# Two rounds of graph message passing on one core: node stages in blocks of 128 nodes instead of 125

## The chip, the cores and the metric

The kernel runs on one core of a Trainium2 chip. The metric is the device time of one execution in microseconds (us), median of the runs shown. The core has five engines that run side by side and wait for each other through semaphores: TensorE (PE in the profile, PEld is its weight load), VectorE (DVE), ScalarE (ACT), GpSimd (POOL) and SyncE (SP, which here only issues transfers). Transfers between the chip's main memory and the on-chip memory of 128 partitions are carried out by the core's 16 DMA engines.

## The reference

`N` = 6250 nodes with 128 features, `E` = 200000 edges sorted by destination.

```
def L0(x):                                   # attention, 4 heads of 32 channels
    xh    = x @ W
    alpha = leaky_relu(xi . a_i + xj . a_j)  # per edge and head, xi = xh[dst], xj = xh[src]
    alpha = softmax of alpha over the edges of one dst
    return segment_sum(xh[src] * alpha, dst)

def L1(x):                                   # three layers, l = 0..2
    h = emb, from layer 1 on normalised over the nodes (gamma, beta)
    w = sigmoid(relu([h[dst], h[src]] @ linA_w.T + linA_b) @ linB_w.T + linB_b)
    prop = segment_sum(w * h[src], dst)
    emb = relu([h, prop] @ lin_w.T + lin_b)
    return emb @ final_w.T + final_b         # after the three layers

x = layernorm(x + L0(x));  return layernorm(x + L1(x))
```

## The kernel before

Two kinds of stages alternate. **Edge stages** walk over 392 groups of 512 edges (`NG` groups, `U` = 8 buffers). For each group POOL issues four indirect gathers of 128 rows of 1 KB each (function `gather`, line 594) from a table in main memory: `T0` (`gat_rows`) in the attention round, `T1` (`mp_rows`) in each of the three layers. SP fetches a window of per-destination data for the group (lines 491 and 548). PE, DVE and ACT work on the group behind them. POOL may be 8 groups ahead: gather `k` waits until group `k - 8` has been used and until ACT has copied its indices (line 669).

**Node stages** walk over the nodes in `N / NB` = 50 blocks of `NB` = 125 nodes, in turns of `BU` = 5 or `BL` = 10 blocks. `node_steps` staggers the sub-steps of a stage over successive blocks, and buffers rotate over 5 slots. A block has its nodes either in the partitions (tiles `[0:NB, ...]`) or in the columns (`[:, ... NB]`). In order of time:

- **Load.** ACT's queue loads `x` into `xall` in five transfers (line 646). SP loads the two edge lists, as 97 partitions of 2048 edges (line 424) and one short row (line 425), and then 23 weight transfers (lines 432 to 449), the last of them parts of `params`. DVE waits for both edge lists (line 892), and computes what the groups need up to line 932; PE waits for all weights before it transposes anything (line 1494), the transposed edge lists go back through DVE (lines 911). Then POOL clears `acc` and `mh` (lines 584, 585), and DVE starts the table stage (line 939).
- **Table of the attention round.** Per block: copy (DVE, line 939), transpose and matmul (PE, 1521 and 1526), copies (ACT 659, 663), results into slot `u` of `tbl` (DVE, 947 to 951), one store of the block's rows to `T0` (SP, line 468), and per turn one store of small rows to `SI` (line 470). The first gather waits for all 50 stores.
- **Normalisation after the attention round.** Here SP loads `x` again by block (`load_x`, line 513) into 5 slots.
- **Per layer, table `T1`.** DVE normalises a block (1299), PE multiplies and transposes it (1637, 1638), ACT and DVE write its rows into `acc` (775, 1306); SP stores five blocks at a time to `T1` (line 527). The first gather of the layer, and ACT in the next stage, wait for all ten stores, since the next stage writes over `acc`.
- **Per layer, table `A3`.** DVE 1316, PE 1648, ACT 789, DVE 1324, ACT 793, DVE 1329; SP stores five blocks at a time to `A3` (`mp_dst_rows`, line 534). When all ten stores have landed, DVE clears `acc` (line 1340) and starts the edge stage. POOL's first 8 groups of gathers run beside this stage.
- **End.** After the third layer 50 blocks are finished, and SP stores each (line 570).

The stores and loads of the node stages have the block's nodes as their first dimension, for example:

```
sp.dma_start(T1[bass.ds(it * (NB * BL) + half * NB * BU, NB * BU), :].rearrange("(b n) c -> n b c", n=NB),
             rows_all[0:NB, row(it, half * BU, TW, 0, BU * TW)].rearrange("n (b c) -> n b c", c=TW))
```

Of the kernel before, what the change touches and what calls it, by code (L numbers as in the profile page):

```python
# [20 lines left out]
P = 128  # L21
T = 4
GE = P * T
W = 32
S = 3
H = 4
U = 8
NB = 125
BU = 5
# [13 lines left out]
PREP_IDENT = 10  # L43
PREP_CONST = PREP_IDENT + 13
PREP_REL = PREP_CONST + 5
# [8 lines left out]
def reached(k0, off, n, done=None):  # L54

    if done is not None and not done["ahead"]:
        return False  # L60
    return not isinstance(k0, int) or k0 + off >= n
# [30 lines left out]
def gnn_kernel(nc, x, src, dst, W0, att, linA_w, linA_b, linB_w, linB_b, lin_w, lin_b, gamma, beta, final_w, final_b,  # L92
# [3 lines left out]
    L = linA_w.shape[0]  # L96
    assert D == P and N % (NB * BU) == 0 and N % (CH * BU) == 0
    CQ = 4
    QP = -(-E // (GE * CQ))
    NG = QP * CQ  # L100
    assert NG % U == 0 and QP <= P and L * 4 * D + D <= U * T * 2 * D - N // NB * D
    QW = GE * CQ
    QF = E // QW
    NT = N // (NB * BU)
    CT = N // (CH * BU)
    NA = N + W
    TW = 2 * D
    AC = max(NA, N // NB * TW // 2)
    C = D // H
# [6 lines left out]

    T0 = nc.dram_tensor("gat_rows", (N, TW), F32, kind="Internal").ap()
    SI = nc.dram_tensor("gat_si", (NA * H, 1), F32, kind="Internal").ap()
    T1 = nc.dram_tensor("mp_rows", (N, TW), F32, kind="Internal").ap()
    A3 = nc.dram_tensor("mp_dst_rows", (NA, S * D), BF16, kind="Internal").ap()  # L120
# [5 lines left out]
    with ExitStack() as ctx:  # L126
        def sb(name, shape, dt=F32):
            return ctx.enter_context(nc.sbuf_tensor(name, shape, dt))

        def sem(name):  # L130
            return ctx.enter_context(nc.semaphore(name))
# [3 lines left out]

        xT = sb("xT", [P, N])
        mh = sb("mh", [P, NA])
        acc = sb("acc", [P, 2, AC])
        hT = mh[:, 0:N]

# [117 lines left out]
        bn = sb("bn", [P, 2])  # L258
        zeros = sb("zeros", [W, H])
        zeros16 = sb("zeros16", [W, S * D], BF16)  # L260

# [16 lines left out]
        more_copied = sem("more_copied")  # L278
        pads_stored = sem("pads_stored")
        acc_cleared = sem("acc_cleared")  # L280
# [91 lines left out]
        def nodes(turn, off, per=BU):  # L372

            return bass.ds(turn * (per * NB) + off * NB, NB)
# [46 lines left out]
        def _(sp):  # L421
            sp.wait_ge(pads_filled, 2)
            for tile, lst in ((dstI, dst), (srcI, src)):
                sp.dma_start(tile[0:QF, :], lst[0:QF * QW].rearrange("(q e) -> q e", e=QW)).then_inc(edges_loaded, 16)
                sp.dma_start(tile[QF:QF + 1, 0:E - QF * QW],  # L425
                             lst[QF * QW:E].rearrange("(q e) -> q e", q=1)).then_inc(edges_loaded, 16)
# [4 lines left out]
            with nc.allow_non_contiguous_dma(reason="columns of small weights"):  # L431
# [13 lines left out]
                for l in range(L):  # L445
                    sp.dma_start(params[:, l, C_LB:C_LB + 1], col(lin_b[l, :])).then_inc(weights_loaded, 16)
                    if l < L - 1:
# [11 lines left out]

            sp.dma_start(A3[N:NA, :], zeros16[:, :]).then_inc(pads_stored, 16)  # L460
            sp.dma_start(SI[N * H:NA * H, :].rearrange("(n h) o -> n (h o)", h=H),
                         zeros[:, :]).then_inc(pads_stored, 16)

            with sp.Fori(0, NT) as it:
# [17 lines left out]
            sp.wait_ge(rel16_stored, 16)  # L483
            sp.wait_ge(pads_stored, 32)
            sp.wait_ge(si_out, 16 * NT)
# [23 lines left out]
            def load_x(turn, off):  # L509
                n, u = turn * BL, off % BU  # L510
                if reached(n, off, BU):
                    sp.wait_ge(ln_y, n + (off - BU + 1))
                sp.dma_start(xrows[0:NB, u, :],
                             x[nodes(turn, off, BL), :]).then_inc(x_in[u], 16)

            sp.wait_ge(gat["acc"], NG)
            node_steps(sp, NT // 2, ((0, load_x),), BL)

# [47 lines left out]

            with sp.Fori(0, NT) as it:
                for u in range(BU):
                    sp.wait_ge(f_out, it * BU + (u + 1))
                    sp.dma_start(out[bass.ds(it * (NB * BU) + u * NB, NB), :],  # L570
                                 xblk[0:NB, u, :]).then_inc(out_done[u], 16)
            for u in range(BU):
                sp.wait_ge(out_done[u], 16 * NT)

        @block.gpsimd
        def _(pool):
            pool.iota(iotaI, pattern=[[1, IW]], base=0, channel_multiplier=0).then_inc(iotas_made, 1)
            pool.iota(pI[:, 0:1], pattern=[[1, 1]], base=0, channel_multiplier=1).then_inc(iotas_made, 1)

            pool.wait_ge(prep, PREP_MORE)
# [61 lines left out]
        def _(act):  # L643

            for n in range(BU):
                act.dma_start(xall[0:NB, n * NT:(n + 1) * NT, :], x[n * NT * NB:(n + 1) * NT * NB, :]
                              .rearrange("(b p) c -> p b c", p=NB)).then_inc(x_in[n], 16)

            for l in range(L):
# [204 lines left out]
        def _(dve):  # L854
# [30 lines left out]
            then(v.memset(negbig[:, :], -BIG))  # L885
            then(v.memset(zeros[:, :], 0.0))
            then(v.memset(zeros16[:, :], 0.0))
            then(v.memset(bn[:, 0:1], 1.0))
# [3 lines left out]

            dve.wait_ge(edges_loaded, 64)
            then(v.tensor_copy(dstF, dstI))
# [60 lines left out]
            for u in range(BU):  # L955
                dve.wait_ge(x_in[u], 16)
            node_steps(dve, NT, ((0, table_x), (3, table_rows)))

# [789 lines left out]
```

## Time and profile before

| what | value |
|---|---|
| median of 3 runs | 8660.34 us (8657.73 to 8661.98) |
| the profiled execution: its own time, its span | 8661.07 us, 8659.3 us |
| busy: PE, DVE, ACT, POOL | 57%, 58%, 16%, 70% of the span |
| mean granted TensorE clock | 0.515 of full speed |
| chain that ended last, by engine | POOL 46%, issue 23%, DMA 11%, DVE 7%, PE 7% |
| moved by DMA | 1075.13 MB, mean 124 GB/s |

Busy shares are averages over stages of different kinds. In the edge stages POOL issues one gather after the other; in the node stages it issues none. The DMA share of a stretch is the mean busy share of the 16 DMA engines, so one engine busy all the time shows as 0.06, and five as 0.31.

### The profile page before, as it was taken

The page shows a single profiled execution, that of the slowest core. Times are in us where ns is not written, and L with a number is a line of the kernel's source. Part 1 is how long each engine was busy: PE and PEld are TensorE (multiplying, and loading weights), DVE is VectorE, ACT ScalarE, POOL GpSimd, SP SyncE. Part 2 cuts the span into 40 slices and gives each one's busy share as a digit, 9 for nine tenths or more (in the row PEclk, how much of TensorE's full clock was granted, in tenths as well). Part 3 has the DMA queues.
Part 4 walks back from the last instruction along what each step waited for, and adds up shares of the span by engine and source line. Part 5 has one row for each costly group of instructions (what it writes and reads, how often), then busy time and mean ns, then how long its engine had stood idle before and what let it go on. Part 6 is the DMA issues. An engine that isn't in the chain of part 4 may idle for free.

```text
span 8659.3 us, 148704 instructions
## 1 busy us (share of the span) xinstructions
PE 4952.0 (57%) x27078; PEld 4216.4 (49%) x27079; DVE 5035.3 (58%) x26803; ACT 1412.8 (16%) x5406; POOL 6049.8 (70%) x6331
## 2 busy tenths in 40 slices
PE   2778788787654455445455554454455545544556
PEld 1667666676644444444444444444444444444445
DVE  4777777777655555555545555555555555555555
ACT  1333333333410000000030000000003000000002
POOL 1777777777367777777737777777773777777774
PEclk7555555555555555555565555555556555555555
DMA  2444444444244444444434444444443444444443
GB/s 77 126 127 128 127 128 127 127 128 127 84 131 130 129 129 130 129 129 130 130 102 127 129 130 130 129 129 130 129 119 110 130 130 129 130 129 129 129 130 93
DMA packets 752117, 1075.13 MB, mean 124 GB/s; under 512 B 323329, under 2 KB 550727, under 8 KB 751531
## 3 DMA queue, kind: packets, MB, share of 16 engines
q0 software_dynamic: 301056, 822.48, 33.0%
q1 hardware_dynamic: 444492, 246.95, 11.3%
q10 hardware_dynamic: 6275, 3.20, 0.1%
q14 instruction: 283, 2.32, 0.1%
q8 instruction: 11, 0.18, 0.0%
HBM read 1027.49 MB, written 44.53 MB: 124 GB/s over the span
## 4 chain that ended last, share of the span: by engine, by line
POOL 46%; issue 23%; DMA 11%; DVE 7%; PE 7%; SPq 2%; DVEq 1%; POOLq 1%; ACT 1%; ACTq 0%
POOL G L594 46%; DMA G<-mp_rows,idx 7%; DMA G<-gat_rows,idx 2%; DVE junk L1376 2%; PE ps L1577 2%; PE ps L1672 1%; PE ps L1537 1%; SPq L534 1%; SPq L527 1%; DMA gat_rows<-ring 1%; DMA mp_rows<-acc 1%; PE ps L1574 0%; SPq L425 0%; PE ps L1564 0%; PE ps L1648 0%
## 5 line engine op out<-in xcount | busy, mean ns | idle before, releaser
L594 POOL DMA_INDIRECT G<-mp_rows,idx x4704 | 4448.6, 946 | 1807.6 <-issue 1323.1
L1672 PE MATMUL ps<-selw,G 128*128 128x32 f32 x9408 | 2222.3, 400 | 596.4 <-DVE selw L1385 595.6
L1672 PEld LDWEIGHTS ps<-selw,G 128*128 128x128 f32 x9408 | 2093.9, 328 | 878.5 <-issue 760.7
L1365 DVE TENSOR_TENSOR pen<-ps,G 128x512 f32<-128x512 f32 x1176 | 812.7, 691 | 2728.2 <-DMA G<-mp_rows,idx 2724.5
L1662 PE MATMUL ps<-awin,ring 96*128 96x128 bf16 x4704 | 715.1, 307 | 2387.0 <-DVE ring L1350 2387.0
L594 POOL DMA_INDIRECT G<-gat_rows,idx x1568 | 1561.7, 996 | 552.6 <-issue 530.7
L1662 PEld LDWEIGHTS ps<-awin,ring 96*128 96x128 bf16 x4704 | 410.1, 132 | 2540.6 <-DVE ring L1350 2540.6
L802 ACT ACTIVATE gate<-logit,cur 128x4 f32<-128x4 f32 x1176 | 349.6, 297 | 5395.0 <-DVE junk L1376 5363.0
L1376 DVE SCALAR_TENSOR_TENSOR junk<-pen,ps 128x128 f32<-128x128 f32 x4704 | 1060.3, 278 | 0.1
L1350 DVE TENSOR_TENSOR ring<-ring,ps 96x512 bf16<-96x512 bf16 x1176 | 795.6, 677 | 0.4
L1577 PE MATMUL ps<-sel,weighted 128*128 128x32 f32 x3136 | 750.8, 404 | 0.0
L1577 PEld LDWEIGHTS ps<-sel,weighted 128*128 128x128 f32 x3136 | 698.0, 327 | 25.3
L1537 PE MATMUL ps<-ident,G 128*128 128x128 f32 x1568 | 428.4, 429 | 333.8 <-DMA G<-gat_rows,idx 332.1
L681 ACT ACTIVATE pen<-ring,negbig 128x512 f32<-128x512 bf16 x392 | 282.8, 721 | 1210.2 <-DVE ring L987 1210.2
L1537 PEld LDWEIGHTS ps<-ident,G 128*128 128x128 f32 x1568 | 280.6, 217 | 355.4 <-issue 207.1
L1013 DVE CUSTOM_DVE_ANT_0 junk<-ps,pen 128x512 f32<-128x512 f32 x392 | 268.1, 684 | 285.1 <-PE ps L1537 144.6
L1376 DVE DVE_READ_ACCUMULATOR junk<-pen,ps 128x1 f32 x4704 | 370.2, 79 | 0.0
L1355 DVE TENSOR_TENSOR ps<-ps,rel_all 128x128 f32<-128x128 f32 x1176 | 335.2, 285 | 0.0
L1385 DVE TENSOR_TENSOR selw<-ps,gate 128x128 f32<-128x128 f32 x1176 | 331.8, 282 | 0.2
L669 ACT COPY idx<-idx_all 128x4 int32 (+1 forms) x1572 | 284.5, 182 | 42.7 <-issue 42.2
L1122 DVE TENSOR_TENSOR weighted<-G,weighted 128x512 f32<-128x512 f32 x392 | 270.6, 690 | 0.0
L697 ACT ACTIVATE weighted<-al 128x512 f32<-128x512 f32 x392 | 246.5, 629 | 104.7 <-DVE al L1093 101.1
(182 smaller groups left out, 5074.3 us busy)
## 6 DMA issues: line engine op xcount, KB each, us to landing
ring<-rel_dst SPq DMA_DIRECT2D x1176, 96.0 KB
G<-mp_rows,idx POOLq DMA_INDIRECT x4704
ring<-rel_dst SPq DMA_DIRECT2D x392, 128.0 KB
awin<-mp_dst_rows SPq DMA_DIRECT2D x1176, 24.0 KB
G<-gat_rows,idx POOLq DMA_INDIRECT x1568
mp_rows<-acc SPq DMA_DIRECT2D x30, 625.0 KB
mp_dst_rows<-acc SPq DMA_DIRECT2D x30, 468.8 KB
sm<-gat_si SPq DMA_DIRECT2D x392, 0.5 KB
```

Of the source, the lines that this page charges most:

```text
L594: pool.indirect_dma_start(out=G[:, u, width * t:width * (t + 1)], out_offset=None, in_=table, in_offset=bass.IndirectOffsetOnAxis(ap=idx[: ...
L669: nc.scalar.copy(idx[:, T * (off % U):T * (off % U) + T], idx_all[:, bass.ds(k0 * T + off * T, T)]).then_inc(idx_ready, 1)
L802: nc.scalar.activation(gate[:, off % 4, :], logit[:, off % 4, :], ACT.Sigmoid, bias=cur[:, C_BB:C_BB + 1]).then_inc(done["gate"], 1)
L1350: v.tensor_tensor(selT16[0:S * W, off % 4, :], relbc16[0:S * W, off % 4, :], nodeP[0:S * W, :].to_broadcast([S * W, GE]), ALU.is_equal).th ...
L1355: v.tensor_tensor(selP[:, off % 4, :].rearrange("p (t n) -> p t n", t=T), iotaP.unsqueeze(1).to_broadcast([P, T, W]), rel4, ALU.is_equal). ...
L1365: v.tensor_tensor(pen[:, off % 2, :].rearrange("p (t c) -> p t c", t=T), PS[off % 2][:, :].rearrange("p (t c) -> p t c", t=T), Grows[:, of ...
L1376: v.scalar_tensor_tensor(junk[:, P * t:P * t + P], pen[:, off % 2, P * t:P * t + P], 0.0, wP, ALU.max, ALU.mult, accum_out=logit[:, off % ...
L1385: v.tensor_tensor(selw[:, off % 4, :].rearrange("p (t n) -> p t n", t=T), one.rearrange("p (t n) -> p t n", t=T), gate[:, off % 4, :].unsq ...
L1537: i = tr(PS[off % 2][:, P * t:P * t + P], Grows[:, off % U, t, D:2 * D], ident[:, :])
L1577: i = mm(PS[4 + b][:, 0:W], R[:, b, D * t:D * t + D], sel[:, off % U, W * t:W * t + W], start=(t == 0), stop=(t == T - 1))
L1662: i = mm(PS[off % 2][:, D * t:D * t + D], selT16[0:S * W, off % 4, P * t:P * t + P], awin[:, off % 4, :], start=True, stop=True)
L1672: i = mm(PS[2 + off % 2][:, 0:W], Grows[:, off % U, t, 0:D], selw[:, off % 4, W * t:W * t + W], start=(t == 0), stop=(t == T - 1))
```

## The change

`NB` becomes 128. The 6250 nodes are padded to `NP` = 6400 = 50 blocks; 48 blocks are full, block 48 has 106 nodes, block 49 none. Tiles and tables that have nodes in their columns or rows grow to 6400. `x` is loaded for 48 blocks as 128 partitions, and for block 48 as 96 and 10 partitions into space that POOL has cleared; in the normalisation stage `load_x` is written out for 50 blocks, and its block 48 waits for the load of its last 10 rows before it is loaded itself. The two edge lists are loaded as 96 partitions, one partition, and the short row. The zero rows behind `A3` and `SI`, two small stores and two DVE fills, are no longer needed. The loop of the last stage's stores is written out, block 48 is stored in two parts, and block 49 is computed and not stored.

```
-NB = 125
+NB = 128
...
-PREP_CONST = PREP_IDENT + 13
+PREP_CONST = PREP_IDENT + 11
...
+    NBLK = 50
+    NP = NB * NBLK
+    NF = N // NB
+    NR = N - NF * NB
+    RS = NR // 16 * 16
...
     QF = E // QW
-    NT = N // (NB * BU)
+    QS = QF // 16 * 16
+    NT = NBLK // BU
     CT = N // (CH * BU)
-    NA = N + W
+    NA = NP
...
-        xT = sb("xT", [P, N])
+        xT = sb("xT", [P, NP])
         mh = sb("mh", [P, NA])
         acc = sb("acc", [P, 2, AC])
...
-                sp.dma_start(tile[0:QF, :], lst[0:QF * QW].rearrange("(q e) -> q e", e=QW)).then_inc(edges_loaded, 16)
+                sp.dma_start(tile[0:QS, :], lst[0:QS * QW].rearrange("(q e) -> q e", e=QW)).then_inc(edges_loaded, 16)
+                sp.dma_start(tile[QS:QF, :], lst[QS * QW:QF * QW].rearrange("(q e) -> q e", e=QW)).then_inc(edges_loaded, 16)
...
-            sp.dma_start(A3[N:NA, :], zeros16[:, :]).then_inc(pads_stored, 16)
-            sp.dma_start(SI[N * H:NA * H, :].rearrange("(n h) o -> n (h o)", h=H),
-                         zeros[:, :]).then_inc(pads_stored, 16)
...
-                sp.dma_start(xrows[0:NB, u, :],
-                             x[nodes(turn, off, BL), :]).then_inc(x_in[u], 16)
+                rows = NB if n + off < NF else RS
+                if n + off == NF:
+                    sp.dma_start(xrows[RS:NR, u, :], x[NF * NB + RS:N, :]).then_inc(x_tail, 16)
+                    sp.wait_ge(x_tail, 48)
+                first = min(n + off, NF) * NB
+                sp.dma_start(xrows[0:rows, u, :], x[first:first + rows, :]).then_inc(x_in[u], 16)
...
-            node_steps(sp, NT // 2, ((0, load_x),), BL)
+            for b in range(NBLK):
+                load_x(b // BL, b % BL)
...
-            with sp.Fori(0, NT) as it:
-                for u in range(BU):
-                    sp.wait_ge(f_out, it * BU + (u + 1))
-                    sp.dma_start(out[bass.ds(it * (NB * BU) + u * NB, NB), :],
-                                 xblk[0:NB, u, :]).then_inc(out_done[u], 16)
+            for b in range(NF):
+                u = b % BU
+                sp.wait_ge(f_out, b + 1)
+                sp.dma_start(out[b * NB:b * NB + NB, :], xblk[0:NB, u, :]).then_inc(out_done[u], 16)
+            sp.wait_ge(f_out, NF + 1)
+            sp.dma_start(out[NF * NB:NF * NB + RS, :], xblk[0:RS, NF % BU, :]).then_inc(out_done[NF % BU], 16)
+            sp.dma_start(out[NF * NB + RS:N, :], xblk[RS:NR, NF % BU, :]).then_inc(out_done[NF % BU], 16)
...
+            nc.gpsimd.memset(xall[:, NF:NBLK, :], 0.0).then_inc(x_pads, 1)
...
-                act.dma_start(xall[0:NB, n * NT:(n + 1) * NT, :], x[n * NT * NB:(n + 1) * NT * NB, :]
+                lo, hi = n * NT, min((n + 1) * NT, NF)
+                act.dma_start(xall[0:NB, lo:hi, :], x[lo * NB:hi * NB, :]
                               .rearrange("(b p) c -> p b c", p=NB)).then_inc(x_in[n], 16)
+            act.wait_ge(x_pads, 1)
+            act.dma_start(xall[0:RS, NF, :], x[NF * NB:NF * NB + RS, :]).then_inc(x_tail, 16)
+            act.dma_start(xall[RS:NR, NF, :], x[NF * NB + RS:N, :]).then_inc(x_tail, 16)
...
-            dve.wait_ge(edges_loaded, 64)
+            dve.wait_ge(edges_loaded, 96)
...
             for u in range(BU):
                 dve.wait_ge(x_in[u], 16)
+            dve.wait_ge(x_tail, 32)
             node_steps(dve, NT, ((0, table_x), (3, table_rows)))
```

## Rows read from the trace of the kernel before

**Rows 1.** Costliest group of the page: busy us, mean ns; idle before it and its releasers.
```profile
L594 POOL DMA_INDIRECT G<-mp_rows,idx x4704 | 4448.6, 946 | 1807.6 <-issue 1323.1
```

**Rows 2.** Waits of POOL over the span: us in total, times, longest us.
```profile
POOL G L594 <- DMA mp_rows<-acc: 272.9, 3, 103.1
POOL G L594 <- ACT idx L669: 221.4, 390, 34.7
POOL acc L584 <- DVE moreI L932: 103.3, 1, 103.3
```

**Rows 3.** POOL's timeline in layer 1: first gather, and ninth group's first.
```profile
4484.14 0.94 POOL L594 DMA_INDIRECT G<-mp_rows,idx  x1 [103.05 <-DMA mp_rows<-acc]
...
4558.76 0.94 POOL L594 DMA_INDIRECT G<-mp_rows,idx  x1 [34.68 <-ACT idx L669]
```

**Rows 4.** Windows of the load stage; last three columns: PE clock, DMA share, GB/s.
```profile
5.00:16.00 11.00, 0.00 (x0) 0.00 (x0) 4.05 (x24) 0.00 (x0) 0.00 (x0) 1.00 0.32 98
...
20.00:30.00 10.00, 0.00 (x0) 0.00 (x0) 0.00 (x0) 0.00 (x0) 0.00 (x0) 1.00 0.06 26
```

**Rows 5.** Windows of layer 1's two table stages, columns as in rows 4.
```profile
4448.00:4453.00 5.00, 4.23 (x28) 3.29 (x27) 4.42 (x21) 4.19 (x21) 0.00 (x0) 1.00 0.34 120
...
4468.00:4473.00 5.00, 0.00 (x0) 0.00 (x0) 0.00 (x0) 0.00 (x0) 0.00 (x0) 0.50 0.34 121
...
4499.00:4504.00 5.00, 4.77 (x15) 3.30 (x14) 4.49 (x22) 3.19 (x14) 3.78 (x4) 0.50 0.64 205
```

**Rows 6.** Issues and median us to landing, from the list of transfers.
```profile
mp_dst_rows<-zeros SPq DMA_DIRECT2D x1, 24.0 KB, 2.2
```

**Rows 7.** Lines of layer 1's table stages (L527: all layers): ns min/median/max, first to last start.
```profile
L527 SPq DMA_DIRECT2D mp_rows<-acc x30: 293/4697/5034, 2330.2 to 6564.5; - x30
L1306 DVE TENSOR_TENSOR acc<-ps,cur x50: 278/286/293, 4424.7 to 4452.3; 125x128 f32 x30, 125x128 f32<-125x128 f32 x20
L1329 DVE TENSOR_TENSOR acc<-ring,acc x50: 278/292/342, 4484.2 to 4517.6; 125x128 f32 x30, 125x128 bf16<-125x128 f32 x20
L1340 DVE MEMSET acc<- x1: 5293/5293/5293, 4543.6 to 4543.6; 128x6282 f32 x1
```

**Rows 8.** Timeline of the load stage: start us, us, engine, line, operation.
```profile
5.22 0.35 SPq L424 DMA_DIRECT2D acc<-in_dst  x1
...
16.74 30.66 SPq L425 DMA_DIRECT2D acc<-in_src  x1
...
75.79 1.23 DVE L894 CAST acc<-acc 98x2048 f32<-98x2048 int32 x1 [65.74 <-DMA acc<-in_src]
...
80.94 0.43 SPq L446 DMA_DIRECT2D params<-in_L_gnn_lin_b  x1
...
85.89 0.45 PE L1494 MATMUL ps<-ident,rhs 128*128 128x128 f32 x1 [85.89 <-DMA params<-in_L_gnn_lin_b]
...
87.48 1.23 DVE L905 CAST acc<-acc 98x2048 f32<-98x2048 int32 x1
...
89.87 3.42 DVE L911 COPY rel_all<-ps 128x392 f32<-128x392 f32 x4 [1.16 <-PE ps L1507]
...
104.55 10.76 POOL L584 MEMSET acc<- 128x12800 f32 x1 [103.30 <-DVE moreI L932]
...
115.25 5.48 POOL L585 MEMSET mh<- 128x6282 f32 x1
```

**Rows 9.** Timeline of the attention round's table stage, and its first gather.
```profile
121.51 3.40 SPq L468 DMA_DIRECT2D gat_rows<-ring  x5
...
121.82 0.29 DVE L947 TENSOR_SCALAR ring<-ps 125x128 f32<-125x128 f32 x1 [0.36 <-PE ps L1526]
...
124.53 0.28 DVE L947 TENSOR_SCALAR ring<-ps 125x128 f32<-125x128 f32 x1
...
195.86 1.10 POOL L594 DMA_INDIRECT G<-gat_rows,idx  x1 [75.13 <-issue]
```

**Rows 10.** Waits of SP in the normalisation stage.
```profile
SPq L513 <- POOL weighted L623: 36.1, 44, 2.4
```

More of the change, by code:

```diff
@@ L96, in gnn_kernel @@
     L = linA_w.shape[0]
-    assert D == P and N % (NB * BU) == 0 and N % (CH * BU) == 0
+    NBLK = 50
[3 more added lines that the diff above has]
+    RS = NR // 16 * 16
+    assert D == P and N % (CH * BU) == 0 and NP >= N + W and (NF, NR) == (48, 106)
     CQ = 4
@@ L100, in gnn_kernel @@
     NG = QP * CQ
-    assert NG % U == 0 and QP <= P and L * 4 * D + D <= U * T * 2 * D - N // NB * D
+    assert NG % U == 0 and QP <= P and L * 4 * D + D <= U * T * 2 * D - NBLK * D
     QW = GE * CQ
     QF = E // QW
-    NT = N // (NB * BU)
+    QS = QF // 16 * 16
+    NT = NBLK // BU
     CT = N // (CH * BU)
-    NA = N + W
+    NA = NP
     TW = 2 * D
-    AC = max(NA, N // NB * TW // 2)
+    AC = max(NA, NBLK * TW // 2)
     C = D // H
@@ L114, in gnn_kernel @@
     NONE16 = 255.0
-    T0 = nc.dram_tensor("gat_rows", (N, TW), F32, kind="Internal").ap()
+    T0 = nc.dram_tensor("gat_rows", (NP, TW), F32, kind="Internal").ap()
     SI = nc.dram_tensor("gat_si", (NA * H, 1), F32, kind="Internal").ap()
-    T1 = nc.dram_tensor("mp_rows", (N, TW), F32, kind="Internal").ap()
+    T1 = nc.dram_tensor("mp_rows", (NP, TW), F32, kind="Internal").ap()
     A3 = nc.dram_tensor("mp_dst_rows", (NA, S * D), BF16, kind="Internal").ap()
@@ L133, in gnn_kernel @@
         PS = [ctx.enter_context(nc.psum_tensor(f"ps{n}", [P, 512], F32)) for n in range(8)]
-        xT = sb("xT", [P, N])
+        xT = sb("xT", [P, NP])
         mh = sb("mh", [P, NA])
         acc = sb("acc", [P, 2, AC])
-        hT = mh[:, 0:N]
+        hT = mh[:, 0:NP]
         dstI = acc[0:QP, 0, 0:QW].bitcast(I32)
@@ L258, in gnn_kernel @@
         bn = sb("bn", [P, 2])
-        zeros = sb("zeros", [W, H])
-        zeros16 = sb("zeros16", [W, S * D], BF16)
         pads_filled = sem("pads_filled")
@@ L278, in gnn_kernel @@
         more_copied = sem("more_copied")
-        pads_stored = sem("pads_stored")
+        x_pads = sem("x_pads")
+        x_tail = sem("x_tail")
         acc_cleared = sem("acc_cleared")
@@ L483, in _ @@
             sp.wait_ge(rel16_stored, 16)
-            sp.wait_ge(pads_stored, 32)
             sp.wait_ge(si_out, 16 * NT)
@@ L510, in load_x @@
                 n, u = turn * BL, off % BU
-                if reached(n, off, BU):
+                if n + off >= BU:
                     sp.wait_ge(ln_y, n + (off - BU + 1))
-                sp.dma_start(xrows[0:NB, u, :],
-                             x[nodes(turn, off, BL), :]).then_inc(x_in[u], 16)
+                rows = NB if n + off < NF else RS
[4 more added lines that the diff above has]
+                sp.dma_start(xrows[0:rows, u, :], x[first:first + rows, :]).then_inc(x_in[u], 16)
             sp.wait_ge(gat["acc"], NG)
-            node_steps(sp, NT // 2, ((0, load_x),), BL)
+            for b in range(NBLK):
+                load_x(b // BL, b % BL)
             with sp.Fori(0, L) as l:
@@ L564, in _ @@
                                  A3[bass.ds(at.node, W), :].rearrange("n (s d) -> (n s) d", s=S)).then_inc(x_win, 16)
-            with sp.Fori(0, NT) as it:
-                for u in range(BU):
-                    sp.wait_ge(f_out, it * BU + (u + 1))
-                    sp.dma_start(out[bass.ds(it * (NB * BU) + u * NB, NB), :],
-                                 xblk[0:NB, u, :]).then_inc(out_done[u], 16)
+            for b in range(NF):
[5 more added lines that the diff above has]
+            sp.dma_start(out[NF * NB + RS:N, :], xblk[RS:NR, NF % BU, :]).then_inc(out_done[NF % BU], 16)
             for u in range(BU):
-                sp.wait_ge(out_done[u], 16 * NT)
+                sp.wait_ge(out_done[u], 16 * (NT + (u == NF % BU) - (u == (NF + 1) % BU)))
         @block.gpsimd
@@ L885, in _ @@
             then(v.memset(negbig[:, :], -BIG))
-            then(v.memset(zeros[:, :], 0.0))
-            then(v.memset(zeros16[:, :], 0.0))
             then(v.memset(bn[:, 0:1], 1.0))
```

## The prediction

> **What bounds the kernel now.** I read the costliest groups first. POOL's gathers lead [rows 1]: (4448.6 + 1323.1) / 4704 = 1.23 us each with their issue gap, back to back. The edge stages run at that pace, and the change alters no gather: as many, of rows as long. What is open is where POOL is not gathering, so the second view is POOL's waits [rows 2]: 273 us for the stores of `T1`, three times; 103 us before its fill at line 584; and inside the 221 us for indices three stalls of up to 34.7 us, one per layer, after the first 8 groups [rows 3]. The third view, the windows, says what holds these stretches. In the load stage the DMA share is 0.06, which is one engine of 16 at 26 GB/s, with every compute engine empty [rows 4]. After the last computation of `T1` it is 0.34 at 121 GB/s with everything else idle [rows 5]: five engines, with a little beside them, about 24 GB/s each. 97 partitions go with one engine, 125 with five. So the node stages wait for transfers that use few engines.
>
> The Trainium skill gives a rule for this ("DMA: Bandwidth & Descriptors", Why a DMA increments its semaphore by 16 and not by 1): a transfer uses the largest number up to 16 that divides the slowest dimension of both sides, hence 1 for 97, 5 for 125, 16 for 128 and 96. The two shares above agree with it.
>
> **How fast the widened transfers can be.** No row shows a 128-partition store of this size. The nearest is the `A3` stage with gathers beside it, share 0.64 at 205 GB/s [rows 5], or 320 GB/s at full share. I take about 350 GB/s for one transfer alone, between that and 16 x 24 = 384; the low bound is 205 GB/s in all, as if nothing went faster than what is seen. By the skill's rule and the row's rate per engine it would be 384, and the sum below less than 1 us smaller. For the fixed part I take the 24 KB store's 2.2 us from issue to landing [rows 6]. Issuing need not shrink to fit: the shortest issue of a five-block store took 0.29 us, the median 4.7 [rows 7], so most of that time is waiting for room in the queue.
>
> **Load stage.** Now SP issues the first list at 5.22, sits in line 425 for 30.66 us, and DVE gets the lists at 75.79. Weights have landed at 85.89; line 911 starts at 89.87, 4.0 later, and POOL's fill at 104.55, 14.7 after that [rows 8]. After the change the six list issues at 0.35 end at 7.3. Then 23 weight transfers: 0.43 unhindered [rows 8]; I take 0.65, since some still meet a full queue: 15.0, to 22.3. The last issue at 80.94 was followed by 4.9 us to PE's start, so weights are there at 27.2. The lists, 1.6 MB beside 3.2 MB of `x`, I put at 14; DVE needs 88.71 - 75.79 = 12.9 for what precedes line 911, to 26.9, so the weights decide: 27.2 + 4.0 + 14.7 = 45.9. Gain 104.55 - 45.9 = **58.7**. Fast bound, every issue 0.43: fill at 40.7, gain 64. Slow bound, all 6.05 MB at 205 GB/s: 31.5 + 4.9 + 4.0 + 14.7 = 55.1, gain 49. POOL's new fill of two blocks at the start, some tenths, and the three short loads of tails lie beside this. POOL's large fills hold DVE's table work until 120.73 [rows 8]; they stay, `mh` with 6400 columns for 6282, **-0.1**.
>
> **Attention table.** From 120.73 to the first gather at 195.86 is 75.1 us [rows 8, 9]. While the five slots were free, DVE's line 947 came every (124.53 - 121.82) / 4 = 0.68 us [rows 9]: that is the pace of the computation. With 16 engines a slot costs 0.72 of DVE's writing, 0.35 of issue, 2.2 + 0.3 of landing, 3.6 for five blocks, 0.72 a block. I take 0.74 for the 47 blocks left, 34.8, plus 2.1 to fill the lags and 3.5 for the last store and POOL's start: 40.4. Gain **34.7**; bounds 37 (0.68 a block) and 25 (0.95, should a landing take 3.6 us).
>
> **Tails of the `T1` stores.** In layer 1 the last block is computed at 4452.3 + 0.3 = 4452.6 [rows 7] and POOL starts at 4484.14 [rows 3]: 31.5 us. The computation itself, 29 us, makes 6.4 MB, or 222 GB/s, less than the stores will take, so only the last store is left: issue 0.3, 655 KB at 350 GB/s 1.9, landing 2.2, POOL 0.1, sum 4.5. Gain 27.0, three layers **81.0**. Bounds: a tail of 10 (205 GB/s from the stage's start) gives 64, one of 3 gives 85.
>
> **Tails of the `A3` stores.** Last block at 4517.9, DVE's fill at 4543.6 [rows 7]: 25.7 us. Afterwards issue 0.3, 492 KB beside the gathers at 230 GB/s 2.1, landing 2.2, and the 1.4 that DVE took to react: 6.0. Gain 19.7, three layers **59.1**. Bounds 13 and 4.5 of tail: 38 and 64. Is it all on the path? POOL's 32 gathers take 39 us from the landing of `T1`. The other way is 33.8 of computation + 6.0 + 15.2 from DVE's fill to POOL's ninth group (4558.76 - 4543.6, [rows 3, 7]), 55. POOL still idles 16, so the gain counts in full. That computation I leave unchanged.
>
> **Small items.** Normalisation: SP waits there for POOL and not the reverse [rows 10], so faster loads gain nothing; block 48 waits for two landings one after the other, some 5.5 us, with about four blocks ahead of it as cover, **-0.5** (0 to -4). SP's window loads queue behind nothing new. DVE and ACT instructions with nodes in the columns get 3 more: under 2.4% of some 0.34 us in seven stages of 50 blocks, **-2.0**. Line 1340 clears 6400 columns for 6282, 0.1 per layer, **-0.3**. The zero stores were off the path, 0. At the end block 49 isn't stored: **+0.5**.
>
> **Sum.** 58.7 + 34.7 + 81.0 + 59.1 + 0.5 - 0.1 - 0.5 - 2.0 - 0.3 = 231.1. The profiled execution took 8661.07 (span 8659.3 and 1.8 around it), 0.7 above the median shown. 8661.07 - 231.1 = **8430**. All fast bounds together: 64 + 37 + 85 + 64 + 1 - 1 = 250, 8411. All slow ones: 49 + 25 + 64 + 38 - 6 = 170, 8491.
>
> **Rivals.**
> - *A ceiling near 205 GB/s for all transfers together.* For it: no window read here is higher. Against it: the share was 0.64 then. The load stage gains 49, the attention table 33, `T1` 64; in the `A3` stage gathers take 105 of the 205 for 39 us, 0.9 MB is left over, and the landing comes 47 instead of 58 us after `T1`'s, 3 x 11 = 33. Sum 179 less 3: **8485**. Chance 0.10.
> - *A few engines drag behind.* The stores now also use engines that so far carried gathers alone, and each waits for its slowest. That costs where gathers run beside stores, in the `A3` stage: with the tail at 13 instead of 6, 3 x 7 = 21, **8451**. The Trainium skill ("DMA: Bandwidth & Descriptors", Latency and other measured facts) says that engines 7 and 15 are usually slower in traces and guesses at GpSimd's descriptor rings as the cause; no row here separates engines. Chance 0.15.
> - *The computation takes less.* Against it: DVE is busy 4.49 of 5 us there. Chance 0.10.
> - *The spreading doesn't happen*, because something else than the number of partitions keeps the transfers on few engines, the lists too. Then only the small costs are left, 8661 + 3 = **8664**. Chance 0.02.
> - *Slower.* Tiles lie elsewhere in the partitions, since `xT`, `mh` and the tables grow. If that made each of the 6272 gathers (4704 and 1568) dearer by 231 / 6272 = 0.037 us, nothing would be left; with 0.05 us the time is 8661 - 231 + 314 = **8744**. Nothing in the rows speaks for it but that POOL's issue is the pace, and any change in it is multiplied. Chance 0.02.
>
> **How the numbers follow.** My forecast, 8430 with its own range of 8411 to 8450, has 0.61; the rivals have the rest. The range 8402 to 8482 takes in the forecast, the drag and the shorter computation, 0.86, less some 0.06 for terms that err together; it leaves out the ceiling at 8485 and the last two. A measurement of this kernel can tell about 0.2%, 17 us. Faster by more has 0.96 (every case but the last two), within 0.02, slower 0.02.
>
> **What would show it.** Load stage: DMA share well above 0.35 from the start, no issue of 30 us in line 425, POOL's fill at 41 to 55 instead of 104.55. Attention table: 38 to 50 us from the end of POOL's fills to the first gather. Each layer: POOL's wait for `T1` down from 103 to about 76 in layer 1, the stall at the ninth group from 34.7 to about 15. Gathers at 1.23 us as before. If the issue of line 527 still takes over 4 us, the spreading or the queue was misread; if gathers change their pace, the sum is off by far more than any term of it.

## The result, and the profile after

| | before | after |
|---|---|---|
| median of 4 runs, us | 8661.16 (8657.73 to 8666.12) | 8411.42 (8406.81 to 8416.44) |
| profiled execution, its span | 8661.07, 8659.3 | 8409.92, 8408.1 |
| ratio | 1 | 0.9711, 95% interval 0.9697 to 0.9726 |

The forecast was 8430. Span against span, 251.2 us went, where the sum had 231.1. Reading both traces stage by stage gives where they went:

| stretch | before | after | gain | forecast |
|---|---|---|---|---|
| start to POOL's fill of `acc` | 104.6 | 45.8 | 58.8 | 58.7 |
| the two fills | 16.2 | 16.3 | -0.1 | -0.1 |
| end of fills to first gather (attention table) | 75.1 | 43.4 | 31.7 | 34.7 |
| attention edge stage | 2059.6 | 2046.9 | 12.7 | 0 |
| `T1` store tails, three | 94.3 | 13.5 | 80.8 | 81.0 |
| `A3` store tails, three | 77.0 | 15.3 | 61.7 | 59.1 |
| everything else | | | 5.5 | -2.3 |

The costliest groups of the page. The layers' gathers are as they were [rows 1]: (4446.8 + 1320.2) / 4704 = 1.23 us. The idle in front of them fell by 145. The second row is the attention round's, 988 ns on average, which in the profile before were 996.
```profile
L603 POOL DMA_INDIRECT G<-mp_rows,idx x4704 | 4446.8, 945 | 1662.3 <-issue 1320.2
L603 POOL DMA_INDIRECT G<-gat_rows,idx x1568 | 1549.0, 988 | 520.9 <-issue 498.9
```
POOL's waits over the span, against [rows 2]: 83 us less for the stores of `T1`, 59 less for indices, 59 less before the fill.
```profile
POOL G L603 <- DMA mp_rows<-acc: 189.8, 3, 75.0
POOL G L603 <- ACT idx L682: 162.1, 398, 14.1
POOL acc L593 <- DVE moreI L943: 44.3, 1, 44.3
```
The load stage, to be read beside [rows 8]. The 30.66 us issue is a 0.28 us one, SP's last weight is issued at 23.78 and not at 80.94, and PE starts at 27.71. Last row: the first gather of the attention round.
```profile
6.69 0.28 SPq L430 DMA_DIRECT2D acc<-in_src  x1
...
18.50 1.23 DVE L905 CAST acc<-acc 98x2048 f32<-98x2048 int32 x1 [8.86 <-DMA acc<-in_src]
...
23.78 0.43 SPq L452 DMA_DIRECT2D params<-in_L_gnn_lin_b  x1
...
27.71 0.45 PE L1506 MATMUL ps<-ident,rhs 128*128 128x128 f32 x1 [27.71 <-DMA params<-in_L_gnn_lin_b]
...
45.78 10.76 POOL L593 MEMSET acc<- 128x12800 f32 x1 [44.28 <-DVE moreI L943]
...
105.46 1.10 POOL L603 DMA_INDIRECT G<-gat_rows,idx  x1 [43.40 <-issue]
```
Windows of the load stage and of layer 1's two table stages, columns as in [rows 4]. In the first two lines the DMA share is above 1, so shares near 1 can't be read as a ceiling; the GB/s can. At 4299 the last rows of `T1` are on their way.
```profile
4.00:6.00 2.00, 0.00 (x0) 0.00 (x0) 1.86 (x6) 0.00 (x0) 0.00 (x0) 1.00 1.16 311
8.00:10.00 2.00, 0.00 (x0) 0.00 (x0) 1.19 (x9) 0.00 (x0) 0.00 (x0) 1.00 1.22 314
...
4299.00:4304.00 5.00, 1.65 (x10) 1.27 (x10) 1.55 (x10) 1.65 (x11) 0.51 (x1) 1.00 0.48 159
4304.00:4309.00 5.00, 4.85 (x16) 3.77 (x16) 4.69 (x26) 3.65 (x16) 3.78 (x5) 0.54 0.51 144
4309.00:4314.00 5.00, 5.00 (x17) 3.74 (x17) 4.46 (x23) 3.43 (x16) 3.78 (x5) 0.50 0.82 243
```
The lines of layer 1's table stages, against [rows 7]: an issue of line 532 takes 0.38 us, not 4.7. DVE's last block of `T1` is at 4298.7 and POOL's first gather at 4303.49, 4.5 after its end. The last block of `A3` is at 4336.9, the clear at 4342.2: 5.0.
```profile
L532 SPq DMA_DIRECT2D mp_rows<-acc x10: 378/383/431, 4274.4 to 4299.2; - x10
L1318 DVE TENSOR_TENSOR acc<-ps,cur x50: 278/290/293, 4271.4 to 4298.7; 128x128 f32 x30, 128x128 f32<-128x128 f32 x20
L1341 DVE TENSOR_TENSOR acc<-ring,acc x50: 281/292/360, 4303.6 to 4336.9; 128x128 f32 x30, 128x128 bf16<-128x128 f32 x20
L1352 DVE MEMSET acc<- x1: 5392/5392/5392, 4342.2 to 4342.2; 128x6400 f32 x1
```
POOL's timeline in layer 1, against [rows 3]: the ninth group waits 13.82 us, not 34.68.
```profile
4303.49 0.94 POOL L603 DMA_INDIRECT G<-mp_rows,idx  x1 [74.82 <-DMA mp_rows<-acc]
...
4357.48 0.94 POOL L603 DMA_INDIRECT G<-mp_rows,idx  x1 [13.82 <-ACT idx L682]
```

### The profile page after: what moved, and what is told of

It reads as the page before. It is cut to its first block, busy times and chain, and to the rows that moved or that the text cites. A ratio compares the mean times of both kernels' runs of the same rounds, so it can differ in the third digit from the quotient of the medians.

```text
span 8408.1 us, 148441 instructions
## 1 busy us (share of the span) xinstructions
PE 4932.5 (59%) x27078; PEld 4196.7 (50%) x27079; DVE 5031.2 (60%) x26801; ACT 1414.8 (17%) x5406; POOL 6035.6 (72%) x6332
## 3 DMA queue, kind: packets, MB, share of 16 engines
q0 software_dynamic: 301056, 822.48, 33.7%
## 4 chain that ended last, share of the span: by engine, by line
POOL 48%; issue 24%; DMA 8%; DVE 8%; PE 8%; DVEq 2%; POOLq 1%; ACT 1%; SPq 0%; ACTq 0%
POOL G L603 48%; DMA G<-mp_rows,idx 6%; DMA G<-gat_rows,idx 2%; DVE junk L1388 2%; PE ps L1589 2%; PE ps L1684 1%; PE ps L1549 1%; PE ps L1660 1%; PE ps L1586 1%; DVEq L987 0%; PE ps L1576 0%; DVE weighted L1134 0%; PE ps L1649 0%; PE ps L1714 0%; PE ps L1715 0%
## 5 line engine op out<-in xcount | busy, mean ns | idle before, releaser
L603 POOL DMA_INDIRECT G<-mp_rows,idx x4704 | 4446.8, 945 | 1662.3 <-issue 1320.2
L682 ACT COPY idx<-idx_all 128x4 int32 (+1 forms) x1572 | 284.3, 182 | 43.2 <-issue 42.9
```

What stands on the lines that cost most here:

```text
L603: pool.indirect_dma_start(out=G[:, u, width * t:width * (t + 1)], out_offset=None, in_=table, in_offset=bass.IndirectOffsetOnAxis(ap=idx[: ...
L682: nc.scalar.copy(idx[:, T * (off % U):T * (off % U) + T], idx_all[:, bass.ds(k0 * T + off * T, T)]).then_inc(idx_ready, 1)
```

## The experiments

They ran on several chips, each used for one set of runs. On some the kernel before takes 8655 to 8661.5 us, as in the first comparison ("the first chip"); on two (here **chip B** and **chip C**) it takes 10690 and 10829. So each time below stands beside the kernel before on the same chip. Expected times were written for the first chip; on B and C their differences and stage times are what is tested. Where a stage is set against the kernel before, that is the first chip's trace, since that kernel as it stands was profiled there alone.

**1. The lists alone.** Blocks of 125, with the list loads of the change (`QS` = 96).

> The kernel before, and of the change only the edge lists as 96 + 1 partitions; x still comes as 125 partitions. Theory (one engine held the lists and the weights behind them): POOL's fill starts at 46 to 50 us instead of 104.55, nothing else moves, 8605 (8600 to 8612). Rival (the five engines of the x load hold the weights as well): fill at 55 to 65, 8612 to 8622. For the attention edge stage (first gather to ScalarE's first copy of the normalisation, 2059.6 us in the trace before, 2046.8 in the one after): if the layout of the tiles in the partitions makes the difference, 2058 to 2061 here, since the layout is that of before; if it is chance in how VectorE and GpSimd meet, anything from 2045 to 2062.

On chip B: 10641.57 us against 10689.83, ratio 0.9953 (0.9937 to 0.9970), -48. POOL's fill starts at 46.7 and the first gather comes at 137.2 instead of 195.9 [rows 9], 58.7 sooner; the time fell by 48, and its interval (32 to 67) holds the 58.7. The attention table (74.3) and the tails of `T1` (31.6 to 31.8) are as before. So 57.8 of the 58.8 of the load stage belong to the lists and would have come without the new blocks.

**2. The blocks alone.** The changed kernel, with the lists as 97 partitions again:
```
-sp.dma_start(tile[0:QS, :], lst[0:QS * QW]...)
-sp.dma_start(tile[QS:QF, :], lst[QS * QW:QF * QW]...)
+sp.dma_start(tile[0:QF, :], lst[0:QF * QW]...)
```

> The changed kernel with the edge lists again as 97 partitions. Theory: the lists are on one engine again, beside a sixteenth of x; 1.75 MB at 26 GB/s, lists there at about 69, POOL's fill at 97, so 51 us above the changed kernel, 8462 (8455 to 8470). Rival (x on 16 engines is what freed the load stage): fill at 46 to 60, 8411 to 8425. Attention edge stage: 2045 to 2048 if the layout decides, 2045 to 2062 if it is chance.

On chip B: 10536.16, ratio 0.9854 (0.9838 to 0.9871). The attention table takes 42.8, the `T1` tails 4.5. The fill starts at 103.4, only 1.2 before the 104.6 of the kernel before; I had expected 97, thinking that the widened loads of `x` would leave the lists more room. SP's issues in the load stage still show the 30 us in the row behind the list:
```profile
18.65 30.63 SPq L430 DMA_DIRECT2D acc<-in_src  x1
```

**3. The `T1` stores on few engines again.** Blocks of 128, but each store cut in two, of 125 and of 3 partitions:
```
+for lo, hi in ((0, 125), (125, NB)):
     sp.dma_start(T1[...].rearrange("(b n) c -> n b c", n=NB)[lo:hi],
                  rows_all[lo:hi, ...]).then_inc(tbl_out[half], 16)
```

> The changed kernel, 128 nodes a block, but each store of T1 in two transfers, partitions 0 to 124 and 125 to 127. Theory (the number of engines decides, not the padding or the block size): five engines carry the stores again, the tail behind the last block goes from 4.6 back to about 31.5 us in each layer, 3 x 27 = 81, 8492 (8488 to 8498). Rival (128 nodes in a block are what made the stores fast): tail 5 to 6 us, 8411 to 8415. Attention edge stage as in blocks_only.

On chip B: 10591.12, ratio 0.9899 (0.9882 to 0.9915). The tails are 34.0, 33.7 and 33.9, some 2 us over the 31.8 of 125 nodes alone; the stores of 3 partitions come on top. POOL's waits, this kernel first, the one of experiment 2 under it:
```profile
POOL G L604 <- DMA mp_rows<-acc: 291.7, 3, 112.6
```
```profile
POOL G L602 <- DMA mp_rows<-acc: 203.5, 3, 83.1
```
88 us for the same rows to the same table. The edit also makes two transfers of each, but in experiment 4 two transfers of 112 and 13 partitions are fast, so it is the partition count. The other stages stay fast (fill at 46.2, `A3` tails 4.6).

**4. No padding, transfers of 112 and 13 partitions.** Blocks of 125 as before, the lists of the change, and every load of `xall` and every store of the three tables cut at 112:
```
+CUTS = ((0, 112), (112, NB))
 ...
+for lo, hi in CUTS:
+    sp.dma_start(T1[...].rearrange("(b n) c -> n b c", n=NB)[lo:hi], rows_all[lo:hi, ...])
```

> The kernel before with blocks of 125 nodes and no padding; the lists as 96 + 1 partitions, and every load and store of a node stage but those of the normalisation and the end as 112 + 13 partitions (16 and 13 engines). Theory: the tails shrink as with 128, 5 us each; SP issues twice as many transfers, so the attention table may be paced by SP at 5.5 us a turn of five blocks instead of 3.85, 16 us more; 8430 (8420 to 8445). Rival (only whole transfers of 128 partitions are fast): tails of 15 us and more, above 8500. Attention edge stage: 2058 to 2061 if the layout decides.

On chip B: 10529.11, ratio 0.9848 (0.9832 to 0.9865). The `T1` tails are 5.1 to 5.5 and those of `A3` 5.0 to 5.1: nearly all of those gains, with 125 nodes in a block. What the padding adds is half as many issues. The attention table takes 67.8 here, against 42.9 in experiment 3. Its row stores, count and ns of one, first to last start:
```profile
L472 SPq DMA_DIRECT2D gat_rows<-ring x100: 310/317/1485, 64.9 to 129.4; - x100
```
100 issues in 64.5 us, 6.4 a turn of five blocks where I had expected 5.5. After its first store SP waits for nothing that the profile shows in this stretch, so SP, not the DMA engines, sets the pace.

The attention edge stage, for which experiments 1 to 4 also had an expectation, takes another time altogether on chip B: 2857.7 and 2860.8 us in experiments 1 and 4 (125 nodes), 2853.0 and 2877.2 in 2 and 3 (128). It doesn't go by the layout there.

**5. The change once more, on a chip of the other kind**, as the base for 6 to 8.

> The changed kernel once more, beside the others of this group. On a chip like that of the first comparison 8411 (ratio 0.971); on one like that of the four kernels before this group, where gathers hold the edge stages and the kernel before takes 10690, the same 200 to 250 us less (ratio 0.977 to 0.981). Attention edge stage: if chance decides, 5 to 20 us off the 2046.8 of the first trace of this kernel on a like chip; if layout and code decide, within 2.

On chip C: 10632.83 against 10829.43, ratio 0.9820 (0.9807 to 0.9834), -197 us where the first chip gave -250. Experiment 6 has the pace of the kernel before, and the two profiles show where some 54 us of the gain stayed away (below).

**6. Only the places of the tiles**, the rival that ends on the slower side. The kernel before, with `xT` and `mh` of 6400 columns; `zeros16` lies in `awin` to make room.
```
-xT = sb("xT", [P, N])
-mh = sb("mh", [P, NA])
+xT = sb("xT", [P, 6400])
+mh = sb("mh", [P, 6400])
```

> The kernel before with xT and mh 6400 columns wide, blocks of 125 as they were (the 24 KB zero tile moved into the window buffer for want of room). Layout theory (the tiles' places make the attention edge stage 12.8 us shorter): that stage as in after_again, time 10 to 15 us under the kernel before. Chance theory, and my rival 'slower by layout' refuted: time within 0.2% of the kernel before, no gather dearer.

On chip C: 10831.8, ratio 1.0003 (0.9993 to 1.0012). Its attention gathers take 946 ns in the median and 987 on average, no more than elsewhere.

**7. The fills cut up.** POOL's two fills of 10.76 and 5.57 us hold DVE. The changed kernel's timeline has four of DVE's copies, later 0.22 us each, stretched over both fills, first all four, then the two that the first fill holds:
```profile
45.86 16.34 DVE L950 TENSOR_SCALAR ring<-G 128x128 f32<-128x128 f32 x4
```
```profile
45.86 10.83 DVE L950 TENSOR_SCALAR ring<-G 128x128 f32<-128x128 f32 x2
```
The Trainium skill ("SBUF — State Buffer", SBUF: two separate sides) says that DVE and GpSimd share a pair of ports, which only some of DVE's instructions use, and that whoever starts first holds it for its whole instruction. The rows agree: two copies end with the first fill (56.69 and 56.55), the other two with the second (62.21 and 62.06). Here each part is filled as soon as nobody needs what lies in it, and the ten stores to `SI` become one:
```
+nc.gpsimd.memset(acc[:, 0, 3 * QW:AC], 0.0).then_inc(acc_cleared, 1)
+nc.gpsimd.memset(acc[:, 1, 2 * QW:AC], 0.0).then_inc(acc_cleared, 1)
+nc.gpsimd.memset(mh[:, QW:NA], -BIG).then_inc(acc_cleared, 1)
...
-nc.gpsimd.memset(acc[:, :, :], 0.0).then_inc(acc_cleared, 1)
-nc.gpsimd.memset(mh[:, :], -BIG).then_inc(acc_cleared, 1)
```

> The changed kernel, with POOL's fill of acc and mh cut in eight, each as soon as its columns are free, and one store of SI at the end of the table stage instead of ten. If POOL's fill holds VectorE's first copies (line 950, four of 4 us), only 3.4 us of it remain behind line 943 instead of 16.3, 12.9 less; if SP paces the table stage (3.85 us a turn, of which 0.9 for SI), that goes to 3.4, 4 less: first gather at about 88 instead of 105.5, time 17 under after_again. Rival (VectorE would be held by something else, or the early fills delay its preparation): under 5.

On chip C: 10617.51, ratio 0.9806 (0.9792 to 0.9819). The first gather comes 18.3 sooner, where I had expected 17: 13.1 from the fills, which end at 49.1 and not at 62.2, and 5.2 from the table, 36.9 for 42.1. The median fell by 15, and the interval overlaps that of experiment 5, so the whole time alone doesn't show it.

**8. And the clear of `acc` shared between ACT and DVE in each layer.**
```
+nc.scalar.activation(acc[:, 0, NA // 2:NA], hT[:, NA // 2:NA], ACT.Identity,
+                     scale=0.0).then_inc(l_clear, 1)
...
-v.memset(acc[:, 0, 0:NA], 0.0).then_inc(l_clear, 1)
+v.memset(acc[:, 0, 0:NA // 2], 0.0).then_inc(l_clear, 1)
```

> clear_early, and in each layer ScalarE clears the upper half of acc beside VectorE (line 1352, 5.39 us). That fill lies on the path to POOL's ninth group: 2.2 us less in each layer, 6 to 7 in all, so 23 to 24 under after_again. Rival (the first window or something else comes last): no difference from clear_early.

On chip C: 10585.08, ratio 0.9785 (0.9771 to 0.9798). This interval lies below that of experiment 5, 0.9807 to 0.9834, so the two edits together are a gain over the change; it overlaps that of experiment 7. ACT takes 2.87 us for its half beside DVE's 2.73, and from the clear to the ninth group it is 12.6 instead of 15.3 us.
```profile
5646.71 2.87 ACT L822 ACTIVATE acc<-mh 128x3200 f32<-128x3200 f32 x1 [3.53 <-DMA mp_dst_rows<-acc]
```
By the profiles the two edits are worth 18.3 + 3 x 2.7 = 26; the clear also starts 3.9 after the last block and not 4.6, 2 more in three layers. The medians are 48 apart. The attention edge stage, which neither edit touches, was 27 and 25 shorter in the profiles of experiments 7 and 8 than in that of 5, and I don't count that as earned.

**9. The change a third time**, base for 10 and 11.

> The changed kernel once more, beside the two below. On a chip like the first it takes 8411 us with 33.7 us from the first gather of a layer to the end of the A3 computation; on a chip like the two others about 10630 us with 66 to 67 us there. Its attention table takes 42 to 43.4 us from the end of POOL's fills to the first gather. If the 12.7 us that the attention edge stage gained is a property of the changed kernel, that stage again takes some 2047 us on a chip like the first; if it is chance, it may come out anywhere between 2045 and 2070.

One run, on a chip like the first: 8415.3 against 8655.28. Attention table 42.4, edge stage 2049.9, from the first gather to the end of the `A3` computation 33.7.

**10. No gathers beside the `A3` stage.** POOL also waits for DVE's clear before a layer's first gather:
```
 pool.wait_ge(tbl_out[half], l * (8 * NT) + 24 * NT)
+pool.wait_ge(l_clear, l + 1)
```

> POOL starts a layer's first gathers only when DVE has cleared acc; nothing is left out. Theory: the gathers beside the A3 stage are what holds its computation, by 5 us idles on the slow chips (66 us) and by contention on the first one (33.7). Then the computation takes about 30 us on any chip. The first 32 gathers (39 us) move behind the clear, so the ninth group comes 40 us after it and not 15: +25 a layer, less the gain in the computation: +21 a layer (+64 in all) on a chip like the first, -11 a layer (-34) on a slow one. Rival: the idles are the chip's own and have nothing to do with gathers; then the computation stays at 66 us there (33.7 on the first), and the time rises by 75 us.

On the same chip: 8499.41, +84. In layer 1 ACT starts on `A3` at 4330.5, and DVE's last block ends at 4364.6: 34.0 us. In experiment 9 the same two points are 34.7 apart (4307.0 to 4341.6); the 33.7 used elsewhere is counted from the first gather. So here the gathers cost that computation 0.6 us, not the 3.7 of the theory. The first gather comes 6.4 us after the clear's start at 4369.2, since that clear takes 5.4, which I had left out of both sums (64 and 75). POOL's wait takes the place of 190.1 us for `T1` and three stalls of 14 at the ninth group, 90 us more in all:
```profile
POOL G L603 <- DVE acc L1354: 322.1, 3, 118.8
```
The attention edge stage was 7.0 shorter than in experiment 9.

**11. One store to `SI` and nothing else**: the second half of experiment 7 by itself.
```
-    sp.dma_start(SI[bass.ds(it * (NB * BU * H), NB * BU * H), :]...)      # in the loop
+sp.dma_start(SI.rearrange("(b n h) o -> n b (h o)", h=H, n=NB),
+             si_all[0:NB, :].rearrange("n (b h) -> n b h", h=H)).then_inc(si_out, 16)
```

> The ten stores to SI, one a turn, become one behind the loop; nothing is left out. Theory: SP's own issues set the pace of the attention table (five row stores and one SI store took 3.84 us a turn where the computation needs 3.4). Then a block takes 0.68 instead of 0.8 us, and the table ends 5 to 6 us sooner: 37 to 38 us from the end of the fills to the first gather instead of 42 to 43. Rival: the slots or the landing of the row stores set the pace; then it stays at 42 to 43. In the whole time that is -5 us or nothing, less than one look tells.

On the same chip: 8411.78, and 37.3 us for the attention table where experiment 9 had 42.4. The row stores, first to last start, the changed kernel's first and this one's under it:
```profile
L469 SPq DMA_DIRECT2D gat_rows<-ring x50: 332/332/645, 62.8 to 102.6; - x50
```
```profile
L469 SPq DMA_DIRECT2D gat_rows<-ring x50: 332/332/1399, 62.8 to 96.5; - x50
```
39.8 / 49 = 0.81 us a block against 33.7 / 49 = 0.69, with slots and the row stores untouched.

**12. Experiment 6 again, for the attention edge stage.**

> The kernel before with xT and mh of 6400 columns, so that the tiles lie where the changed kernel has them, once more, for the 12.7 us that the attention edge stage took less after the change (2059.5 to 2046.8 us, and 2049.9 in a second profile), all of it in the mean length of the attention gathers (996 ns before, 988 and 990 after). If the place of the tiles is the cause, this kernel on a chip like the first shows gathers of about 989 ns, an edge stage of about 2048 us, and takes 8649 us instead of 8661. If it is something else in the change (the tables' 6400 rows, or when the stage starts), it shows 996 ns, 2060 us and 8661. On a chip like the two slow ones the question can't be seen: 2912 us and a ratio of 1.000, as before.

On another chip like the first: 8662.32 against 8661.5, ratio 1.0 (0.999 to 1.0009). Its edge stage took 2063.6, its gathers 999 ns:
```profile
L594 POOL DMA_INDIRECT G<-gat_rows,idx x1568 | 1565.7, 999 | 553.0 <-issue 531.6
```
So the place of the tiles is not what shortened that stage.

## Why the prediction was right, and where its terms were off

**What bounds the kernel: right.** Node stages waited for transfers that used few engines, by the partition count. Experiment 3 takes the wide transfers from one table, and 29 us of waiting a layer come back; experiment 4 gives wide transfers to blocks of 125, and the tails go. The Trainium skill's rule ("DMA: Bandwidth & Descriptors", Why a DMA increments its semaphore by 16 and not by 1) agrees with what is seen: shares of 0.06 at 97 and 0.34 at 125 partitions, windows of 311 and 314 GB/s with 128 and 96, tails of 5.1 to 5.5 with 112 and 13. No row here counts the engines themselves.

**Load stage: right, 58.8 for 58.7, and so close by luck.** PE starts at 27.71 (forecast 27.2), but SP issues the last weight at 23.78, not 22.3, and PE starts 3.9 after that, not 4.9. The lists, put at 14, came at 18.50. In the sum DVE would be ready at 26.9 and wait for PE until 31.2; in fact it has no pause before line 922:
```profile
30.22 1.23 DVE L916 CAST acc<-acc 98x2048 f32<-98x2048 int32 x1
...
31.48 3.41 DVE L922 COPY rel_all<-ps 128x392 f32<-128x392 f32 x4
```
Lists and weights were ready together there. In the profiles of experiments 1, 5 and 9 DVE waits 1.8, 0.3 and 0.6 us for PE at this place, so the weights decide, as I said, but by far less than the 4 us of my sum.

**Attention table: mis-sized, 31.7 for 34.7.** The term that was off is "I take 0.74 for the 47 blocks left": I took the computation's pace of 0.68 and left SP a part-time role. SP's timeline in the changed kernel:
```profile
84.76 2.67 SPq L469 DMA_DIRECT2D gat_rows<-ring  x5
87.66 0.39 SPq L471 DMA_DIRECT2D gat_si<-weighted  x1
88.59 2.72 SPq L469 DMA_DIRECT2D gat_rows<-ring  x5
```
Issues of 0.33 us start (2.67 - 0.33) / 4 = 0.59 us apart, and with the store to `SI` a turn takes 88.59 - 84.76 = 3.83 us of SP, 0.77 a block. At 0.69 a block, as in experiment 11, my 0.74 would have been enough. The price of an issue was right; the issues per block and what SP does between them were not counted. That is 47 x 0.03 = 1.4 of the 3.0 missing. Another 1.9 lie in a single turn, in which DVE waited 2.0 us for the slot of a store:
```profile
79.04 4.58 SPq L469 DMA_DIRECT2D gat_rows<-ring  x5
```
The other two profiles of this kernel (experiments 5 and 9) have shorter stops near this place and tables of 42.1 and 42.4; the cause is open.

**`T1` tails: right in sum**, 4.5 each for 4.5, 80.8 for 81.0, with two terms off that cancel. A store lands 3.3 us after its issue (last column), where I had 0.3 + 1.9 + 2.2 = 4.4; but POOL starts 1.0 after the landing, not 0.1.
```profile
mp_rows<-acc SPq DMA_DIRECT2D x30, 640.0 KB, 3.3
mp_dst_rows<-acc SPq DMA_DIRECT2D x30, 480.0 KB, 3.3
```

**`A3` tails: right within 2.6**, 5.0 to 5.3 each for 6.0. The landing was mis-sized here too, 3.3 for 0.3 + 2.1 + 2.2 = 4.6, and DVE's reaction takes 1.5 for 1.4. The ninth group still waited 13.8 us, so the gain counted in full, as argued.

**Small items: wrong in sign, by 8 in all.** I charged 2.8 for wider columns, block 48 and the clear. The clear's 0.1 a layer shows (5.39 for 5.29), and line 1318's median is 290 ns for 286 before. But the normalisation takes 69.9 for 70.3, and the node and edge stages of the layers and the end came out 5.1 shorter together. Of these, 2.7 lie between the ninth group and the last gather of a layer (1919.0 for 1919.9), and experiment 9 doesn't repeat them (1920.1). I can't assign the rest.

**Attention edge stage: counted as 0, measured 12.7.** The step is "the change alters no gather". Medians are equal, 946 ns, in both kernels, but some gathers take up to 1.47 us. Over 1.05 us are 183 of 1568 in the profile before and 189 in experiment 12; in the changed kernel 147, 157 in experiments 9 and 11, 140 in 10. Beyond 0.946 us each they hold 71.1 us before and 58.0 after: that is the 12.7. So it came four times out of four on chips like the first, against two profiles of kernels with 125 nodes. It isn't the place of tiles (experiment 12). On chip C it is absent (2911.6 in experiment 6, 2913.2 in experiment 5), and the count goes the other way: 166 long gathers with 125 nodes, 191 to 193 in the three changed kernels. On chip B it is 162 and 159 with 125, 153 and 148 with 128. So whether this gain belongs to the change at all isn't shown. What makes a gather long stays open; the 6400 rows of the tables and the moment at which the stage starts weren't tried by themselves.

**The rivals.** *A ceiling near 205 GB/s* fell: windows of 311 and 314 GB/s, `T1` tails of 4.5. *A few engines drag* fell: with gathers beside them, stores of `A3` end 5.0 to 5.3 after the last block. *The computation takes less* fell: the granted clock was 1.00 up to 4304, 0.54 in the next window and 0.50 after it, though PE was busy 4.85 of 5 us there; the computation took 33.7 us as before, and 0.6 less without any gathers. Its 8418 lies nearer to the measured 8411.42 than my 8430, so the time alone would have spoken for the wrong rival; the stage times don't. *The spreading doesn't happen* and *slower by the layout* fell, the latter by experiments 6 and 12. What the forecast missed, 20.1, had no rival: 12.7 of the edge stage, 7.8 of the small items, 2.6 of the `A3` tails, less 3.0 of the table. Most of it is unexplained: the measured time sits at the sum of all fast bounds, 8411, though of the four large terms only `A3` came out clearly on that side.

**Why the gain is smaller on chip C.** Per stage, experiment 6 against 5: up to the first gather 196.2 to 104.4 (-91.9, the first chip -90.4), `T1` tails -81.7 (-80.8), but from the first gather of a layer to the clear, three layers, 239.5 to 213.9: -25.6, where the first chip had 178.1 to 116.5, -61.6. There the `A3` computation takes 66 to 68 us, not 33.7, with either kernel. The stores have longer to drain, the tail before was 12.3 and not 25.7, and it falls to 4.6 all the same. So a tail is worth its backlog: what the stores fall behind during the computation, not how slow they are. That is 36 of the 54; 14 more are the edge stage, -12.7 there and +1.6 here.

## What to carry to other kernels

Look at the DMA share of a window in which all engines are empty: 0.06 or 0.34 where only one kind of transfer runs means one or five engines, and the remedy is the number of partitions that one transfer spans. Padding to 128 and cutting at a multiple of 16 both do it; the cut doubles the issues, and once a block's transfer is fast, the issuing queue (0.33 us each here, 0.77 a block with its loop) is next in line. Size a tail as the backlog at the end of the computation, and take it from the kind of chip on which the kernel will run.

## What the runs showed of the hardware that was not expected

**Two kinds of chips.** The same kernel before took 8655 to 8661.5 us in three sets of runs and 10690 and 10829 in two, each within 0.4%. The four sets of the experiments ran on four chips, each chip at one time only, so that it is the chip, and not what went on around it at that time, isn't shown. Gathers are as long there (945 ns); what grows is POOL's idle time. The costliest group of experiment 5, and POOL's waits:
```profile
L603 POOL DMA_INDIRECT G<-mp_rows,idx x4704 | 4447.5, 945 | 3009.3 <-issue 1366.8
```
```profile
POOL G L603 <- ACT idx L682: 1051.4, 232, 46.8
POOL G L603 <- remote: 900.0, 267, 4.1
```
In the `A3` stage there, PE, DVE and ACT each stand still for 3.4 to 5.3 us at a time, all three together for 2.4 to 3.8, while POOL goes on. Windows of experiment 5, a normal one and two of these, and what DVE's line 1341 waited for:
```profile
5620.00:5625.00 5.00, 4.74 (x17) 3.56 (x16) 4.71 (x25) 3.63 (x17) 3.78 (x5) 0.56 0.44 122
...
5639.00:5644.00 5.00, 0.62 (x2) 0.33 (x2) 0.00 (x0) 0.46 (x2) 3.78 (x5) 0.50 0.66 203
5650.00:5655.00 5.00, 0.36 (x2) 0.06 (x1) 0.35 (x2) 0.47 (x2) 3.79 (x4) 0.50 0.36 105
```
```profile
  issue: 29.5, 10
```
For nearly all of these pauses the profile names no releaser but "issue" or "remote". Experiment 10 was meant to tell whether the gathers cause them, and met a chip without them; the cause is open.

**The clock fell although the gap was closed.** TensorE's granted clock was 1.00 (2.4 GHz) in the later part of layer 1's `T1` stage and in the window from 4299, in which PE was busy 1.65 of 5 us, with the gap between the stages only 4.5 us long. From 4304 it was 0.54 on average and then 0.50 (1.2 GHz): it fell near 4304.4, some 0.9 us after the next stage's first gather. In the kernel before it fell in the long gap: up to 4453 it was 1.00 [rows 5], and the next 5 us have 0.74, so it fell some 2.4 us into them.
```profile
4453.00:4458.00 5.00, 0.91 (x8) 0.71 (x7) 0.11 (x1) 0.00 (x0) 0.00 (x0) 0.74 0.34 121
```
What made it fall with the gap closed isn't shown.
